# Last attention of a four-layer transformer: fewer unread products at its front, and a new order of ScalarE's work

## The reference

```python
# y: the conditioned x; prev is the token before (zero at the first)
xk, xv, xr = (y * mix_n + prev(y) * (1 - mix_n) for n in (k, v, r))
k, v, r = xk @ Wk.T, xv @ Wv.T, xr @ Wr.T
sr = sigmoid(r)
# rwkv_linear_attention, one step per token, for each feature:
#   out_t = (e1 * a + e2 * v_t) / (e1 * b + e2)
#   where top = running maximum, e1 = exp(top - max(top, first + k_t)),
#         e2 = exp(first + k_t - max(top, first + k_t))
#   a, b = kept1 * a + kept2 * v_t,  kept1 * b + kept2, likewise against the new maximum
x = x + (sr * out) @ Wo.T
```

## Time and profile before

| | |
|---|---|
| median of 3 runs | 1290.98 us (1289.88 to 1291.87) |
| the profiled execution, its own time | 1292.66 us |
| its span, first to last instruction | 1290.8 us |
| mean granted TensorE clock, share of full | 0.976 |
| TensorE busy | 1206.6 us, 93% |
| VectorE busy | 923.9 us, 72% |
| ScalarE busy | 659.5 us, 51% |
| GpSimd busy | 520.9 us, 40% |

### The profile page before, as it was taken

The page is one execution under the profiler, slowest core; times in us unless marked ns, Lnnn a source line. Parts: engine busy times, 40 slices in busy tenths (PEclk is TensorE's granted clock), DMA queues, the critical chain, the costliest instruction groups (busy, mean ns, idle before and its releaser), DMA issues. The chain is left out here.

```text
span 1290.8 us, 17019 instructions
## 1 busy us (share of the span) xinstructions
PE 1206.6 (93%) x5978; PEld 846.0 (66%) x5978; DVE 923.9 (72%) x1822; ACT 659.5 (51%) x1511; POOL 520.9 (40%) x423
## 2 busy tenths in 40 slices
PE   7989999999999999999799998999999978599998
PEld 2445656565567766333478875999999943268876
DVE  8867677675867997952634335999999997963355
ACT  3267777666746555445244425444444447252344
POOL 1068677676603221530073330555555530415520
PEclk9989999999989999999899998999999999799999
DMA  2122122121011102300535422111111000011102
GB/s 99 37 74 58 50 58 62 46 50 33 18 42 40 42 21 83 117 1 1 209 112 198 151 89 89 34 34 34 33 34 34 13 1 32 1 53 55 41 29 66
DMA packets 31940, 73.42 MB, mean 57 GB/s; under 512 B 5443, under 2 KB 15172, under 8 KB 29297
## 3 DMA queue, kind: packets, MB, share of 16 engines
q1 hardware_dynamic: 29280, 67.44, 17.0%
q0 software_dynamic: 1536, 3.86, 1.0%
q10 hardware_dynamic: 1040, 1.05, 0.2%
HBM read 55.89 MB, written 6.29 MB: 48 GB/s over the span
## 5 line engine op out<-in xcount | busy, mean ns | idle before, releaser
L186 POOL TENSOR_TENSOR sums<-scans 128x512 f32<-128x512 f32 x56 | 75.5, 1348 | 301.4 <-DVE scans L169 192.2
L593 POOL TENSOR_TENSOR probs<-probs,stats 128x512 f32<-128x512 f32 x64 | 83.9, 1311 | 105.5 <-DVE stats L765 105.4
L655 ACT ACTIVATE probs<-ps_s,stats 128x256 f32<-128x256 f32 (+1 forms) x256 | 104.4, 426 | 29.2 <-DVE stats L759 28.9
L203 DVE RECIPROCAL sums<-sums 128x256 f32<-128x256 f32 x56 | 97.4, 1740 | 21.5 <-POOL sums L191 21.5
L759 DVE CUSTOM_DVE_ANT_0 ps_s<-ps_s,mask 128x256 f32<-128x256 f32 (+1 forms) x256 | 83.2, 386 | 24.4 <-PE ps_s L891 24.1
L191 POOL TENSOR_TENSOR sums<-sums,terms 128x512 f32<-128x512 f32 x56 | 76.0, 1357 | 4.4
L2135 PE MATMUL K_ps_kvp<-K_wqkv_hi,K_xin_hi 128*128 128x256 f32 x256 | 74.7, 292 | 0.0
L867 PE MATMUL ps_p<-xin,wkvq 128*128 128x512 f32 x144 | 69.9, 609 | 4.3 <-ACT qraw L644 2.3
L1085 POOL TENSOR_TENSOR L3hid<-L3hid,L3sig 128x1024 f32<-128x1024 f32 x17 | 46.1, 2716 | 68.3 <-DVE L3hid L1193 37.8
L662 ACT ACTIVATE probT<-ps_t 128x768 f32<-128x768 f32 x64 | 52.2, 816 | 40.0 <-PE ps_t L902 40.0
L2135 PE MATMUL K_ps_kvp<-K_wqkv_lo,K_xin_hi 128*128 128x256 f32 x256 | 72.3, 282 | 0.0
(11 more groups left out here) (420 smaller groups left out, 3535.2 us busy)
## 6 DMA issues: line engine op xcount, KB each, us to landing
E_fc<-l_fc_dram SPq DMA_DIRECT2D x16, 1024.0 KB, 7.4
qswap<-qraw SPq DMA_DIRECT2D x60, 128.0 KB, 2.3
ahead<-l_wqkv_dram SPq DMA_DIRECT2D x16, 384.0 KB, 3.3
L3wgu<-L_w_dram SPq DMA_DIRECT2D x17, 256.0 KB, 2.6
L0wgu<-L_w_dram SPq DMA_DIRECT2D x14, 256.0 KB, 2.7
L3wdn<-L_w_dram SPq DMA_DIRECT2D x17, 128.0 KB, 2.0
wkvq<-w_l0a_dram SPq DMA_DIRECT2D x4, 512.0 KB, 4.0
wo<-w_l0a_dram SPq DMA_DIRECT2D x4, 512.0 KB, 3.6
```

Source lines behind the costliest of these rows:

```text
L186: pstep.mark(pool.tensor_tensor(sums[:, k, :, :], scans[:, k, :, 0, :], scans[:, k, :, 1, :], ALU.add))
L203: dstep.mark(dve.reciprocal(den, den))
L593: pool.tensor_tensor(p1, p1, rs[:, 0:2].unsqueeze(2).to_broadcast([P, 2, T]), ALU.mult)
L655: ins = act.activation(dst[:, i % 2, :], src[:, i % 2, :], ACT.Exp, bias=stats[:, g % 4, 4 + i:5 + i], scale=-1.0, accum_out=stats[:, g % ...
```

## The change

TensorE's seven unread products at the stage's front become four. ScalarE's order becomes: copies 0 to 3 (k of both chunks), kept terms of chunk 0, copies 4 and 5 (v of chunk 0), out terms of chunk 0, copies 6 and 7 (v of chunk 1), kept terms of chunk 1, sigmoid copies 8 to 11 (r), out terms of chunk 1, and then one `next_sigmoid`. VectorE waits, ahead of each chunk's `grow`, for `evac` >= 2 ch + 6 as well as for the kept terms.

```diff
--- before.py
+++ after.py
@@ -2317,19 +2317,29 @@
                     act.activation(dst[:, ch, half(h)], ps[:, g % 8, :], ACT.Sigmoid if g >= 8 else ACT.Identity) \
                         .then_inc(s["evac"], 1)
 
-                for g in range(8):
+                def terms_of(ch, j):
+                    act.wait_ge(s["diff_ready"], 2 * ch + j + 1)
+                    diff, other = (keep1, keep2) if j == 0 else (out2, out1)
+                    act.activation(other[:, ch, :], diff[:, ch, :], ACT.Relu)
+                    astep.link(act.activation(diff[:, ch, :], diff[:, ch, :], ACT.Relu, scale=-1.0))
+                    act.activation(keep1[:, ch, :] if j == 0 else out1[:, ch, :],
+                                   keep1[:, ch, :] if j == 0 else out1[:, ch, :], ACT.Exp, scale=-1.0)
+                    act.activation(keep2[:, ch, :] if j == 0 else out2[:, ch, :],
+                                   keep2[:, ch, :] if j == 0 else out2[:, ch, :], ACT.Exp, scale=-1.0).then_inc(s["exp_ready"], 1)
+
+                for g in range(4):
                     evac(g)
-                for ch in range(CH):
-                    for j, pair in enumerate(((keep1, keep2), (out1, out2))):
-                        act.wait_ge(s["diff_ready"], 2 * ch + j + 1)
-                        diff, other = pair if j == 0 else pair[::-1]
-                        act.activation(other[:, ch, :], diff[:, ch, :], ACT.Relu)
-                        astep.link(act.activation(diff[:, ch, :], diff[:, ch, :], ACT.Relu, scale=-1.0))
-                        for x in pair:
-                            ins = act.activation(x[:, ch, :], x[:, ch, :], ACT.Exp, scale=-1.0)
-                        ins.then_inc(s["exp_ready"], 1)
+                terms_of(0, 0)
+                evac(4)
+                evac(5)
+                terms_of(0, 1)
+                evac(6)
+                evac(7)
+                terms_of(1, 0)
                 for g in range(8, 12):
                     evac(g)
+                terms_of(1, 1)
+                next_sigmoid(act, l + 1)
                 for n in range(3):
                     added_act(act, l + 1, n)
 
@@ -2364,6 +2374,7 @@
                                              op0=ALU.add, op1=ALU.subtract).then_inc(s["diff_ready"], 1)
                 for ch in range(CH):
                     dve.wait_ge(s["exp_ready"], 2 * ch + 1)
+                    dve.wait_ge(s["evac"], 2 * ch + 6)
                     dstep.link(dve.tensor_tensor(grow[:, ch, :], keep2[:, ch, :], v[:, ch, :], ALU.mult))
                     for b in range(NB):
                         c = slice(b * T, (b + 1) * T)
@@ -2393,7 +2404,7 @@
 
             @block.tensor
             def _(pe):
-                unread_products(pe, ps[:, 7, :], 7)
+                unread_products(pe, ps[:, 7, :], 4)
                 pe.wait_ge(s["ld_w"], 16)
                 for g in range(16):
                     j, m, h = g // 4, g // 2 % 2, g % 2
```

## The result

| | before | changed |
|---|---|---|
| median | 1290.98 us (1289.88 to 1291.87, 5 runs) | 1284.78 us (1282.62 to 1286.97, 5 runs) |
| ratio to before | | 0.9946, 95% interval 0.9931 to 0.9962 |
| the profiled execution: own time, span | 1292.66, 1290.8 us | 1286.97, 1284.9 us |
| up to the last attention | 1064.5 us | 1066.5 us |
| the last attention | 69.72 us | 62.80 us |

The forecast was 1284.4 us, and 6.6 us less in this stage; the stage has lost 6.92 us. The two spans differ by 5.9 = 6.9 + 0.9 - 2.0: beyond the 6.9 of the stage, 0.9 were gained in the last stage and 2.0 lost ahead of the changed one, in code that is the same in both. So the spans alone understate what the change did to its stage.

A forecast was written before the change was run, and what follows sets the result against it. The prediction took VectorE's chain in the last attention to bound the kernel. Terms 1.3 + 4.3 + 1.0 = 6.6 us took the median from 1290.98 to 1284.4 us, range 1282.5 to 1287.6, 79 in 100 for the forecast.

The forecast's parts named there:

- The carrier: Last attention: VectorE, dense between its waits, carries the chain; TensorE is not the limit there.
- The front: Start of the last attention: three unread products fewer let VectorE's scans begin 1.3 us earlier, at most 1.8.
- The wait for kept terms: VectorE ahead of chunk 0's `grow`: its 4.34 us wait for ScalarE's kept terms goes, 4.3 us gained.
- the spare of 0.9: Chunk 0's `grow`: copies 4 and 5 end 0.9 us before VectorE is free; each microsecond later costs one.
- The wait for GpSimd: VectorE after chunk 0's reciprocal: earlier r copies shrink its 1.29 us wait for GpSimd by 1.0 us.
- `next_sigmoid`: ScalarE's idle stretch: loads the Sigmoid tables early; without it the load would cost 1.28 us at the finished quarters.
- The drain of the Trainium skill: ScalarE's table loads: the skill adds about 1.38 us of drain, 2.66 per switch; GpSimd's spare would fall to 1.6.
- The rival of half-clock spells: Output product or behind the router: one to two half-clock spells cost 1.6 us each, 1286.0 to 1287.6; 13 in 100.
- The rival "slower": Last attention's groups: full clock not granted after the shorter front, r copies late, 1298.4 us; 2 in 100.

The follow-up runs named there:

- e4: Changed kernel with copies 4 and 5 (v of chunk 0) behind the out terms of chunk 0 instead of ahead: stage 65.9 us, against 62.80 for the changed kernel.
- e6: Changed kernel with the four r copies behind all terms, two table loads instead of four and no `next_sigmoid`: stage 63.9 us, against 62.80.
- the repeat: Changed kernel once more, unedited, beside the kernel before on one chip: stage 62.81 us, ratio to before 0.9953.
- e5: Changed kernel without `next_sigmoid`, the one-column Sigmoid behind the last terms: stage 62.8 us, one run.
- e3: Changed kernel with no unread products at the front: stage 64.3 us, against 62.80 for the changed kernel.
- e1: Kernel before with four unread products at the front instead of seven, nothing else: stage 67.60 us, against 69.72 before.
- e2: Changed kernel with seven unread products at the front again, so ScalarE's new order alone: stage 64.24 us, against 69.72 before.
- b3: Changed kernel with chunk 1's reciprocal on ScalarE as exp(-ln(den)), VectorE making numerator and products, GpSimd idle in chunk 1: stage 60.6 us.
- b4: Kernel of b3 with chunk 0 done the same way, so GpSimd has no work in the stage: stage 60.1 us.
- b1: Changed kernel with the product of out term and v of both chunks on GpSimd instead of VectorE: stage 64.9 us, against 62.80.
- b2: Kernel of b1 with GpSimd starting the numerator when its scans are done, not the denominator: stage 71.6 us.
- b5: Kernel of b4 with chunk 1's first product and numerator scans in VectorE's wait for chunk 0's reciprocal, and fewer middle unread products: stage 58.1 us.

## Why the prediction was right, step by step

The carrier was named rightly: VectorE, by its waits. The terms of the sum and what they measured, from each stage's start:

- The front, forecast 1.3: first scan at 10.64 in place of 12.11, 1.47. The 0.17 more come from ScalarE's two k copies, which ran together from 1075.94 to 1077.00, the first starting 0.09 before the small Exp ended. The groups started 5.57 us after the stage's start, forecast 5.4. That `mixed` and not the front sets this start holds too: in the kernels with eight front instructions these took from 3.67 to 5.37 us, and the groups began 5.6 us after the start each time.
- The wait for kept terms, forecast 4.3: gone whole, 4.34, and 0.08 more as `grow` now overlaps the instruction before it. e4 shows the spare of 0.9.
- The wait for GpSimd, forecast 1.0: 1.29 to 0.26, 1.03. e6, with the r copies last, has it at 1.38, so their place decides it.
- In sum 1.47 + 4.34 + 0.08 + 1.03 = 6.92, forecast 6.6.
- That the median of the whole, 1284.78 us, fell within 0.4 of the forecast 1284.4 is in part luck: the runs spread over 4.4 us, and in the repeat the medians lay 4.1 apart, not 6.6. The stage lengths, 62.80 and 62.81, are what bears the sum out.
- `next_sigmoid`, forecast to save 1.28: wrong, it saves nothing (e5). The step that failed is that the load would wait with its sigmoid for the finished quarter. It stood outside the sum, so the forecast didn't suffer.
- The drain of the Trainium skill (ScalarE: Activation LUTs, What ACT_TABLE_LOAD costs), 1.38 us at each switch, shows in no load of this stage; the measurement decides.
- The rival of half-clock spells: a spell of 3.4 us in the last stage, near the router, as before; none at the output product. Its price, half of a spell's length, isn't borne out in the last stage: over the 14 profiles the clock stood at half there for 3.4 us in six and for 6.8 in eight, and the stage took 155.6 to 158.0 us in the six and 156.5 to 157.2 in the eight. What makes this stage longer or shorter was not taken apart.
- The rival "slower" had the whole 14 us above the forecast: e3, the strongest form of it, lost 1.5 us.

## What to carry to other kernels

Find the engine that is dense between its waits, and follow the new order forward from its stage's start with one row for each kind of instruction; here that gave e1, e2, e4 and e6 within some 0.1 us, and b3 and b4 too. It missed where an engine's instruction took a length that no row had shown (b1, b2, beside GpSimd) and where a load did not wait as assumed (e5). Gains of two parts don't add when both shorten one wait: measure each alone and both. Before handing a dense VectorE's work to an idle engine, look at what that engine's other work does to VectorE: here ScalarE left its products at 0.69 us for 128x512, and GpSimd cost more than it saved.

## What the runs showed of the hardware that I had not expected

- Beside GpSimd's tensor products VectorE's instructions that read two tensors nearly stop: four scans 2.41 us alone, 4.54 beside one product of 2.79, 8.41 beside three. GpSimd's products of this size grow too, from 2.17 us to between 2.34 and 2.79. The 1.49 us of the product at 1118.19 in the changed kernel (0.69 alone, at 1122.98) is the same effect, 0.8 us that stand in both kernels (1.49 at 1123.15 before).
- ScalarE's table load doesn't wait for what its activation waits for: it ended 19.7 us ahead in e5, and 9.6 us ahead of the Ln in b3.
- The clock at the front varies with the run. In b1 and b5 TensorE had stood 2.05 and 2.04 us ahead of the front, the clock stayed at full, and the eight instructions took 3.67 us, 0.43 each. In the other eleven profiles with a front it had stood 3.08 us; there the clock fell to half between 0.6 us ahead of the first front product and 0.8 after it, and rose 2.8 to 4.2 us after it. The stage length doesn't follow this: 62.8 us in the changed kernel and in e5, where the clock fell at different moments.
